# A four-layer selective scan on one core: the gates of a chunk go from VectorE to ScalarE and GpSimd, and the preparation of later chunks gets a new order

## The chip, the cores and the metric

One core of a Trainium2 chip runs the whole program. The metric is the device time of one execution in microseconds (us), the median of three runs. Five engines work side by side, each in the order of its own instruction stream: TensorE (PE, with its weight loads PEld), VectorE (DVE), ScalarE (ACT), GpSimd (POOL) and SyncE (SP), which here issues all DMAs. They are tied together by semaphores only: an instruction that raises a count, and waits for a count ahead of another instruction.

## The reference

The input is 4 sequences of 2048 tokens with 256 features, all in float32. It is normalised, sent through four Mamba layers, added to the input, and sent through a feed-forward part whose operands are quantised to FP4 in blocks. One Mamba layer computes:

```python
xs, z = split(x @ in_w.T)                    # 2 x 512 channels
xc = silu(cb + causal_conv4(xs, cw))
dt, Bm, Cm = split(xc @ xp_w.T)              # 16, 16, 16 columns
delta = softplus(dt @ dt_w.T + dt_b)
h[t] = h[t-1] * exp(delta[t] * A) + (delta[t] * xc[t]) * Bm[t]     # 512 channels x 16 states
y[t] = sum over states of h[t] * Cm[t] + xc[t] * D_skip
x = layer_norm((y * silu(z)) @ out_w.T + x)
```

## The kernel before, in words

**Chunks and steps.** A layer is cut into 16 chunks of 512 tokens (four for each sequence), so the four layers are 64 chunks, counted on as g = 0 to 63. The 512 x 16 states of a chunk are worked in 16 *steps* s = 0 to 15. A step holds four tiles of 128 partitions (32 channels x 4 states) by 512 tokens, and four steps (QS) together give all 16 states of one block of 128 channels, called q. In step s:

- ScalarE, a step ahead, makes `dA` = exp(delta x A) for step s+1 (`exp`, L629), after it has kept the last column of step s-1 (`keep_states`, L638);
- TensorE spreads the B rows over the partitions into the one PSUM bank `B_all` (`broadcast_b`, L456), for step s+1, once VectorE has written both halves of `bu` of step s;
- VectorE multiplies `durep` by `B_all` into `bu` (`times_b`, L1018, two of 1024 columns) and runs four hardware scans (`scan`, L1033). Its order in a step is scan 0, `times_b` second half, scans 1 and 2, `times_b` first half of the next step, scan 3;
- GpSimd multiplies the four states by the C rows into `hc` (`times_c`, L905, two of 1024 columns). `h` and `hc` hold two steps, so the scan of step s+2 waits for `times_c` of step s;
- TensorE, two steps behind, adds `hc` over the states into the PSUM bank `acc` (`sum_states`, L474). In the first step of a block it opens the bank with `skip_term` (L463), the product of `xc` and D_skip, and for that waits until the bank has been read (`acc_read`).

**The gate.** When the four steps of a block are summed, VectorE multiplies `acc` by silu(z) (`gate`, L1039, 128x512). It stands behind scan 0 of steps 6, 10 and 14, and of step 2 of the next chunk.

**The preparation.** Beside these, the engines prepare the chunk to come (n = g+1) and the one after that (g+2), and finish the one before (g-1). Which piece stands in which step is written out by hand in `turn` of each engine. TensorE: last convolution of n in step 0, `project_x` 2, `project_dt` 3 and 4, `project_out` of g-1 5 and 6, `project_in` for z 8 and 9, `transpose_x` of g+2 10, `project_in` for xs 11 and 12, convolutions 13 to 15. ScalarE follows a step later: in steps 0 and 1 the last copies of the convolution, tanh and silu(z), in 4 and 5 the two linear halves of softplus and the sigmoid, in 6 a polynomial (`polynomial`, L724 to L727) that ends with `quad`. GpSimd then has four products of 128x2048: `softplus` 0 (L917) in step 7, 1 (L920) in 8, 2 (L923, gives delta) in 10 and 3 (L927, gives du = delta x xc) in 11. Pieces that pass through the PSUM banks W[0] and W[1] are numbered by `fill`; `w_filled` and `w_read` count by these numbers.

**The transfers.** SP issues, in written order, a store of delta and one of du (1 MB each) to DRAM, and then the loads that replicate their rows over 128 partitions: `load_delta` (into `drep`) and `load_du` (into `durep`, both L309), 4 DMAs of 256 KB for each block q, two blocks in the memory at a time. Block 0 of the next chunk is used by VectorE at the end of step 15 (`times_b` of the next chunk's step 0). `load_x` (L258) brings the tokens of g+2 into the part of `xc` that blocks 0 and 1 of chunk g use, after a step of `sum_states` that shows that they are no longer read.

Of the kernel before, what the change touches and what calls it, by code (L numbers as in the profile page):

```python
# [55 lines left out]
def mamba_layers(nc, x, xbuf, wguT_dram, wdT_dram, w, NL, L, sem):  # L56
# [12 lines left out]
    C_DB, C_CB = 0, DB  # L69

# [7 lines left out]
    with ExitStack() as ctx:  # L78
        def sb(name, shape, dt=F32):
# [79 lines left out]
        acc_read, row_summed, mean_ready, squared, var_ready, lnv_done, guess_ready, newton, root_done, normed, weighted, x_ready = (  # L159
            sem(n) for n in ("acc_read", "row_summed", "mean_ready", "squared", "var_ready", "lnv_done", "guess_ready", "newton",  # L160
# [31 lines left out]
        def outs(n):  # L192

            return 1 if not isinstance(n, int) or n >= 2 else 0

        def fill0(n, name):

            base = 11 * n + 3 if outs(n) else 5 + 10 * n
            if isinstance(n, int) and n == TOT:
                return base - 5  # L200
            return base + {"xp": 0, "dt1": 1, "dt3": 2, "out": 3, "z0": 3 + outs(n), "z2": 4 + outs(n), "tr": 5 + outs(n),
                           "xs0": 6 + outs(n), "xs2": 7 + outs(n), "c0": 8 + outs(n), "c2": 9 + outs(n)}[name]

        def fill1(n, name):

            base = 10 * n + 2 if outs(n) else 4 + 9 * n
            if isinstance(n, int) and n == TOT:
                return base - 4
            return base + {"c3": 0, "dt0": 1, "dt2": 2, "out": 3, "z1": 3 + outs(n), "z3": 4 + outs(n), "tr": 5 + outs(n),
                           "xs1": 6 + outs(n), "xs3": 7 + outs(n), "c1": 8 + outs(n)}[name]  # L210

        FIRST = {"tr": 0, "xs0": 1, "xs1": 1, "xs2": 2, "xs3": 2, "c0": 3, "c1": 3, "c2": 4}

        def fill(b, n, name):

            if name in FIRST:
                if isinstance(n, int) and n == 0:
                    return FIRST[name]
                n = n - 1
            return (fill0, fill1)[b](n, name)  # L220

        LAST_OUT = (fill0(TOT, "out") + 1, fill1(TOT, "out") + 1)

        def out_fill(b, m):

            if isinstance(m, int) and m == TOT - 1:
                return LAST_OUT[b]
            return fill(b, m + 2, "out")
# [19 lines left out]
        def _(sp):  # L248
# [196 lines left out]
        def _(pe):  # L445
# [12 lines left out]
            def skip_term(n, p_, q):  # L458
                if q == 0:
                    pe.wait_ge(skip_w, 16 * layer_of(n) + 16)  # L460
                if positive(DB * n + q):
                    pe.wait_ge(acc_read, DB * n + q)
                pe.matmul(acc[:], skip[:, q, :], xc[:, p_, q, :], start=True, stop=False, skip_group_check=True)  # L463

            def sum_states(at, p_):
# [3 lines left out]
                if s % QS == 0:  # L469
                    skip_term(n, p_, s // QS)  # L470
                for k in range(4):
                    if k % 2 == 0:
                        pe.wait_ge(hc_ready, 2 * G + k // 2 + 1)
                    ins = pe.matmul(acc[32 * k:32 * k + 32, :], gather[:], hc[:, 4 * (s % 2) + k, :], start=False,  # L474
# [97 lines left out]
            for e in range(3):  # L572
# [42 lines left out]
        def _(act):  # L615
# [123 lines left out]

            def squares(m):  # L740
                act.wait_ge(mean_ready, m + 1)
                if positive(m):
# [76 lines left out]
            for e in range(2):  # L819
# [6 lines left out]
            def turn(g, ph):  # L826
                here = ph % 2
                n, other = g + 1, 1 - here
                for s in range(NG):
                    keep_states(group(g, s - 1))  # L830
                    exp(group(g, s + 1), here if s + 1 < NG else other)
                    if not is_last(g):
                        if s == 0:
                            copy_conv(n, other, 2)
                            take_params(n, other)
                        if s == 1:
                            copy_conv(n, other, 3)
                            tanh_xc(n, other)
                    if s == 1:
# [17 lines left out]
                    if not is_last(g):  # L857
                        if s == 9 and is_first(g):
                            act.wait_ge(weights_saved, 48)
                        if s in (9, 10):  # L860
                            copy_z(n, other, 2 * (s - 9))
                            copy_z(n, other, 2 * (s - 9) + 1)
# [5 lines left out]
                    if not is_last(g):  # L868
                        if not (isinstance(g, int) and g == TOT - 2):
                            if s == 11:  # L870
                                copy_xT(g + 2)
                            if s in (12, 13):
# [891 lines left out]
```

## Time and profile before

| what | value |
|---|---|
| median of 3 runs | 8295.75 us (8295.15 to 8297.27) |
| profiled execution | 8298.0 us, span 8296.2 us |
| PE / DVE / ACT / POOL busy | 79% / 95% / 67% / 84% |
| granted TensorE clock, mean | 0.894 of full |
| 64 chunks (first gate at 178.01 us, last at 7564.45 us) | about 116 us a chunk |
| feed-forward part behind them | from about 7600 us to the end |

A row of the timeline begins with its start in us from the span's start and its duration; "x2" behind it means two instructions merged into one row. Neighbouring instructions of an engine overlap a little in the records, so what one costs is read as the distance between starts. Idle time ahead of an instruction stands in brackets with what ended it. Most rows are from chunk 33, whose step 5 begins at 3999.98 us.

### The profile page before, as it was taken

How to read it: one execution, taken by the hardware profiler on the slowest of the kernel's cores; microseconds unless marked ns; L12 is line 12 of the kernel's file. 1: busy time of each engine (PE TensorE's matmuls, PEld its weight loads, DVE VectorE, ACT ScalarE, POOL GpSimd, SP SyncE). 2: the span in 40 equal slices, each digit the busy share in tenths (PEclk: the TensorE clock that was granted, in tenths of full speed). 3: DMA queues.
4: the chain of work that ended last, by engine and by line, in shares of the span. 5: the costliest groups of instructions: out<-in, count | busy, mean ns of one | idle time of the engine just before them, and what ended most of it. 6: DMA issues, size and time to landing. Idle time of an engine off the chain costs nothing. (4 is left out here: it accounts for less than half of the span.)

```text
span 8296.2 us, 75437 instructions
## 1 busy us (share of the span) xinstructions
PE 6530.6 (79%) x21028; PEld 2528.0 (30%) x21028; DVE 7849.2 (95%) x7411; ACT 5545.2 (67%) x9589; POOL 6983.9 (84%) x3444
## 2 busy tenths in 40 slices
PE   5777777787778777787777877887777877775888
PEld 2222222232223222222222322232222322222555
DVE  8999999999999999999999999999999999996776
ACT  5676776777766776667766777667766777663444
POOL 3898889988898888988899888988889888985555
PEclk8989899989989899898999889898999888987999
DMA  6454454444554454554545445454555445451110
GB/s 181 116 118 109 104 127 115 117 115 113 127 118 110 100 121 115 120 122 108 126 115 117 105 109 126 116 125 103 121 119 119 109 104 122 115 118 52 39 38 30
DMA packets 566028, 909.25 MB, mean 110 GB/s; under 512 B 58368, under 2 KB 200192, under 8 KB 564352
## 3 DMA queue, kind: packets, MB, share of 16 engines
q1 hardware_dynamic: 565632, 904.73, 45.7%
q8 instruction: 156, 2.56, 0.1%
q14 instruction: 240, 1.97, 0.1%
HBM read 715.55 MB, written 188.94 MB: 109 GB/s over the span
## 5 line engine op out<-in xcount | busy, mean ns | idle before, releaser
L905 POOL TENSOR_TENSOR hc<-h,crep 128x1024 f32<-128x1024 f32 x2048 | 4782.2, 2360 | 714.3 <-PE acc L474 633.4
L1033 DVE TENSOR_TENSOR_SCAN h<-dA,carry,bu 128x512 f32<-128x512 f32 x3072 | 3755.0, 1264 | 0.4 <-ACT carry L638 0.4
L1018 DVE TENSOR_TENSOR bu<-durep,B_all 128x1024 f32<-128x1024 f32 x2048 | 2480.8, 1211 | 188.2 <-PE B_all L456 168.2
L629 ACT ACTIVATE dA<-drep,cur 128x512 f32<-128x512 f32 x4096 | 2618.7, 711 | 0.6 <-DMA drep<-delta_dram 0.3
L456 PE MATMUL B_all<-dtc,spread_b 128*128 128x512 f32 x2048 | 1308.0, 724 | 1460.8 <-DVE bu L1018 1458.5
L638 ACT COPY carry<-h 128x4 f32<-128x4 f32 x1023 | 199.4, 195 | 1713.0 <-DVE h L1033 1711.6
L474 PE MATMUL acc<-hc,gather 128*32 128x512 f32 x8192 | 1284.9, 703 | 5.5 <-POOL hc L905 5.5
L1033 DVE TENSOR_TENSOR_SCAN h<-dA,bu 128x512 f32<-128x512 f32 x1024 | 1192.4, 1203 | 6.9 <-ACT dA L629 6.8
L498 PE MATMUL work<-xT,inw 128*128 128x512 f32 x2048 | 1119.6, 697 | 93.1 <-ACT xT L649 82.7
L456 PEld LDWEIGHTS B_all<-dtc,spread_b 128*128 128x128 f32 x2048 | 360.0, 208 | 2144.9 <-DVE bu L1018 2057.0
L508 PE MATMUL work<-xs,taps 128*128 128x512 f32 x2048 | 950.3, 607 | 0.0
L498 PEld LDWEIGHTS work<-xT,inw 128*128 128x128 f32 x2048 | 438.2, 226 | 868.0 <-issue 855.8
L508 PEld LDWEIGHTS work<-xs,taps 128*128 128x128 f32 x2048 | 369.1, 190 | 586.0 <-issue 586.0
L536 PE MATMUL work<-outw,sz 128*128 128x256 f32 x2048 | 485.9, 380 | 0.0
L474 PEld LDWEIGHTS acc<-hc,gather 128*32 128x32 f32 x8192 | 171.7, 115 | 934.8 <-issue 731.6
L917 POOL TENSOR_TENSOR quad<-quad,xs 128x2048 f32<-128x2048 f32 x64 | 289.1, 4516 | 170.2 <-ACT quad L727 170.2
L536 PEld LDWEIGHTS work<-outw,sz 128*128 128x128 f32 x2048 | 392.6, 192 | 55.2
L1373 PE MATMUL f_gu<-f_wguT,f_xqT 128*128 128x512 f32 (+1 forms) x768 | 346.6, 605 | 73.5 <-ACT f_xqT L1453 66.5
L910 POOL TENSOR_TENSOR xc<-xc,quad 128x2048 f32<-128x2048 f32 x64 | 289.9, 4530 | 44.3 <-ACT quad L694 44.3
L463 PE MATMUL acc<-xc,skip 128*128 128x512 f32 x512 | 322.8, 718 | 0.0
L927 POOL TENSOR_TENSOR relu<-za,xc 128x2048 f32<-128x2048 f32 x64 | 290.8, 4544 | 0.1
L920 POOL TENSOR_TENSOR quad<-quad,za 128x2048 f32<-128x2048 f32 x64 | 290.7, 4542 | 0.1
(179 smaller groups left out, 6807.8 us busy)
## 6 DMA issues: line engine op xcount, KB each, us to landing
drep<-delta_dram SPq DMA_DIRECT2D x1024, 256.0 KB, 6.4
durep<-du_dram SPq DMA_DIRECT2D x1024, 256.0 KB, 7.2
crep<-c_dram SPq DMA_DIRECT2D x1024, 64.0 KB, 6.7
delta_dram<-za SPq DMA_DIRECT2D x64, 1024.0 KB, 4.2
du_dram<-relu SPq DMA_DIRECT2D x64, 1024.0 KB, 5.3
x_res<-xbuf SPq DMA_DIRECT2D x64, 512.0 KB, 3.8
xbuf<-x_res SPq DMA_DIRECT2D x64, 512.0 KB, 5.4
xc<-xbuf SPq DMA_DIRECT2D x63, 512.0 KB, 4.3
```

The lines of the kernel that those rows point to most:

```text
L456: pe.matmul(B_all[:], spread_b[:, s % QS, :], dtc[:, p_, :], start=True, stop=True).then_inc(bb_ready, 1)
L463: pe.matmul(acc[:], skip[:, q, :], xc[:, p_, q, :], start=True, stop=False, skip_group_check=True)
L474: ins = pe.matmul(acc[32 * k:32 * k + 32, :], gather[:], hc[:, 4 * (s % 2) + k, :], start=False, stop=s % QS == QS - 1, skip_group_check=True)
L498: ins = pe.matmul(W[b][:], inw[:, k, z * DI + e * P:z * DI + (e + 1) * P], xT[:, k, :], start=k == 0, stop=k == KD - 1)
L508: ins = pe.matmul(W[b][:], taps[:, 4 * e + k, :], xs[:, e, k:k + T], start=k == 3, stop=k == 0)
L536: ins = pe.matmul(half, sz[:, p_, k, t * P:(t + 1) * P], outw[:, k, :], start=False, stop=k == DB - 1)
L629: act.activation(dA[:, 4 * (s % 2) + k, :], drep[q % 2][:, k, :], ACT.Exp, scale=cur[:, p_, 4 * s + k:4 * s + k + 1]).then_inc(da_ready, 1)
L905: pool.tensor_tensor(hc[:, pair, :], h[:, pair, :], crep[:, j:j + 1, :].to_broadcast([P, 2, T]), ALU.mult).then_inc(hc_ready, 1)
L927: pool.tensor_tensor(relu[:], za[:], xc[:, p_], ALU.mult).then_inc(du_ready, 1)
L1018: dve.tensor_tensor(bu[:, 2 * k:2 * k + 2, :], durep[q % 2][:, 2 * k:2 * k + 2, :], B_all[:].unsqueeze(1).to_broadcast([P, 2, T]), ALU.mul ...
L1033: dve.tensor_tensor_scan(h[:, r, :], dA[:, r, :], bu[:, k, :], start, ALU.mult, ALU.add).then_inc(scanned, 1)
L1373: ins = pe.matmul(gu[:, at:at + width], xqT[:, t % 2, k, :], wguT[:, k, at:at + width], start=k == 0, stop=k == KD - 1)
```

## The change

Three things change. The gate leaves VectorE: ScalarE copies `acc` into `sums` (`take_sums`) and GpSimd multiplies it by silu(z) from there (its own `gate`, counted by `gated`). The term with D_skip no longer opens the bank; it is added in another step of the block (`SKIP_AT`). The preparation of n and g+2 moves by one step on TensorE (convolution 3 from step 0 to 15 of the turn before, z to 7 and 8, transposes to 9, xs to 10 and 11) and on ScalarE and, for `silu_xc`, on GpSimd; `load_x` waits for a later step of `sum_states`, since block 1 is now read up to step 7. The fill numbers are now counted out in the new order. Cut to its core:

```diff
+    SKIP_AT = (1, 3, 1, 1)
...
             def load_x(n):
-                    sp.wait_ge(summed, 2 * (NG * (n - 2) + QS) + 1)
+                    sp.wait_ge(summed, 2 * (NG * (n - 2) + 2 * QS - 1) + 1)
...
             def load_skip(layer, n):
-                    sp.wait_ge(summed, 2 * NG * n - 6)
+                    sp.wait_ge(summed, 2 * NG * n - 3)
...
             def skip_term(n, p_, q):
-                if positive(DB * n + q):
-                    pe.wait_ge(acc_read, DB * n + q)
-                pe.matmul(acc[:], skip[:, q, :], xc[:, p_, q, :], start=True, stop=False, skip_group_check=True)
+                pe.matmul(acc[:], skip[:, q, :], xc[:, p_, q, :], start=False, stop=False, skip_group_check=True)
...
             def sum_states(at, p_):
-                if s % QS == 0:
-                    skip_term(n, p_, s // QS)
+                q = s // QS
+                if s % QS == 0 and positive(DB * n + q):
+                    pe.wait_ge(acc_read, DB * n + q)
+                if s % QS == SKIP_AT[q]:
+                    skip_term(n, p_, q)
...
             def project_out(m, p_, j):
-                    pe.wait_ge(acc_read, DB * (m + 1))
+                    pe.wait_ge(gated, DB * (m + 1))
...
             def turn(g, ph):     # TensorE
-                        if s == 0:
-                            convolve(nxt, 3)
...
-                        if s in (8, 9):
-                            project_in(nxt, 2 * (s - 8), 1)
-                            project_in(nxt, 2 * (s - 8) + 1, 1)
+                        if s in (7, 8):
+                            project_in(nxt, 2 * (s - 7), 1)
+                            project_in(nxt, 2 * (s - 7) + 1, 1)
-                            if s == 10:
+                            if s == 9:
                                 transpose_x(g + 2)
-                            if s in (11, 12):
-                                project_in(g + 2, 2 * (s - 11), 0)
-                                project_in(g + 2, 2 * (s - 11) + 1, 0)
-                            if s in (13, 14, 15):
-                                convolve(g + 2, s - 13)
+                            if s in (10, 11):
+                                project_in(g + 2, 2 * (s - 10), 0)
+                                project_in(g + 2, 2 * (s - 10) + 1, 0)
+                            if s >= 12:
+                                convolve(g + 2, s - 12)
...
+            def take_sums(n, q):     # ScalarE
+                act.wait_ge(summed, 2 * (NG * n + QS * (q + 1)))
+                if positive(DB * n + q - 1):
+                    act.wait_ge(gated, DB * n + q - 1)
+                squares_ahead = n if q in (1, 2) else n - 1 if q == 0 else min(n, TOT - 1)
+                if positive(squares_ahead):
+                    act.wait_ge(squared, squares_ahead)
+                act.copy(sums[:, q % 2, :], acc[:]).then_inc(acc_read, 1)
...
             def turn(g, ph):     # ScalarE
                     keep_states(group(g, s - 1))
+                    if s == 10 and not is_last(g) and g < TOT - 2:
+                        copy_xT(g + 2)
+                    if s == 2 and not is_first(g):
+                        take_sums(g - 1, DB - 1)
+                    if s in (6, 10, 14):
+                        take_sums(g, (s - 6) // 4)
                     exp(group(g, s + 1), here if s + 1 < NG else other)
                         if s == 0:
-                            copy_conv(n, other, 2)
+                            copy_conv(n, other, 3)
                             take_params(n, other)
-                        if s == 1:
-                            copy_conv(n, other, 3)
                             tanh_xc(n, other)
-                    if s == 1:
+                    if s == 0:
...
                         silu_z(g, here)
...
-                        if s in (9, 10):
+                        if s in (8, 9):
                             copy_z(...)
...
-                            if s in (12, 13):
+                            if s in (11, 12):
                                 copy_xs(...)
...
-                            if s in (14, 15):
-                                copy_conv(g + 2, here, s - 14)
+                            if s >= 13:
+                                copy_conv(g + 2, here, s - 13)
...
+            def gate(n, p_, q):     # GpSimd
+                if q == 0:
+                    pool.wait_ge(z_done, n + 1)
+                pool.wait_ge(acc_read, DB * n + q + 1)
+                pool.tensor_tensor(sz[:, p_, q, :], sums[:, q % 2, :], sz[:, p_, q, :], ALU.mult).then_inc(gated, 1)
...
             def turn(g, ph):     # GpSimd
-                        if s == 2:
+                        if s == 1:
                             silu_xc(g + 1, other)
...
                     times_c(group(g, s))
+                    if s == 2 and not is_first(g):
+                        gate(g - 1, other, DB - 1)
+                    if s in (6, 10, 14):
+                        gate(g, 1 - other, (s - 6) // 4)
...
             def turn(g, ph):     # VectorE
                     scan(at, ph, 0)
-                    if s == 2 and not is_first(g):
-                        gate(g - 1, other, DB - 1)
-                    if s in (6, 10, 14):
-                        gate(g, here, (s - 6) // 4)
                     times_b(at, 1)
```

## Rows read from the trace of the kernel before

**Rows 1.** Costliest groups by line, shapes apart: busy us, mean ns | idle before

```profile
L905 POOL TENSOR_TENSOR hc<-h,crep 128x1024 f32<-128x1024 f32 x2048 | 4782.2, 2360 | 714.3 <-PE acc L474 633.4 <-DMA wdT_dram<-sz 40.3 <-DVE h L1033 34.7
...
L1039 DVE TENSOR_TENSOR sz<-acc,sz 128x512 f32<-128x512 f32 x256 | 170.6, 666 | 6.1 <-PE acc L474 6.1
```

**Rows 2.** Who waited for whom, on VectorE, whole span: total us, times, longest us

```profile
DVE bu L1018 <- PE B_all L456: 168.2, 177, 3.1
...
DVE bu L1018 <- DMA durep<-du_dram: 18.6, 24, 7.7
```

**Rows 3.** Busy time by engine, chunks 32 to 35 (four together)

```profile
sum 465.00, PE 370.40 PEld 136.13 DVE 453.51 ACT 327.37 POOL 414.26; mean PE 92.60 PEld 34.03 DVE 113.38 ACT 81.84 POOL 103.57
```

**Rows 4.** Timeline of VectorE, chunks 32 and 33: start us, us, what

```profile
3961.47 1.23 DVE L1018 TENSOR_TENSOR bu<-durep,B_all 128x1024 f32<-128x1024 f32 x1 [0.22 <-DMA durep<-du_dram]
...
3998.80 2.44 DVE L1033 TENSOR_TENSOR_SCAN h<-dA,carry,bu 128x512 f32<-128x512 f32 x2
...
4002.28 2.44 DVE L1033 TENSOR_TENSOR_SCAN h<-dA,carry,bu 128x512 f32<-128x512 f32 x2
...
4008.11 0.67 DVE L1039 TENSOR_TENSOR sz<-acc,sz 128x512 f32<-128x512 f32 x1
4008.70 1.22 DVE L1018 TENSOR_TENSOR bu<-durep,B_all 128x1024 f32<-128x1024 f32 x1
...
4064.58 2.44 DVE L1033 TENSOR_TENSOR_SCAN h<-dA,carry,bu 128x512 f32<-128x512 f32 x2
...
4077.97 1.21 DVE L1018 TENSOR_TENSOR bu<-durep,B_all 128x1024 f32<-128x1024 f32 x1
...
4107.01 1.23 DVE L1018 TENSOR_TENSOR bu<-durep,B_all 128x1024 f32<-128x1024 f32 x1 [0.56 <-PE B_all L456]
...
4115.10 2.44 DVE L1033 TENSOR_TENSOR_SCAN h<-dA,carry,bu 128x512 f32<-128x512 f32 x2
```

**Rows 5.** Timeline of ScalarE, steps 5 to 10

```profile
4000.11 0.20 ACT L638 COPY carry<-h 128x4 f32<-128x4 f32 x1 [2.00 <-DVE h L1033]
...
4017.99 1.99 ACT L727 ACTIVATE quad<-quad,quad_rest 128x2048 f32<-128x2048 f32 x1
...
4020.68 2.56 ACT L629 ACTIVATE dA<-drep,cur 128x512 f32<-128x512 f32 x4
...
4038.63 1.04 ACT L732 COPY sz<-work 128x512 f32<-128x512 f32 x2
```

**Rows 6.** Timeline of GpSimd, steps 7 to 12

```profile
4020.12 4.52 POOL L917 TENSOR_TENSOR quad<-quad,xs 128x2048 f32<-128x2048 f32 x1 [2.32 <-ACT quad L727]
...
4038.50 9.32 POOL L905 TENSOR_TENSOR hc<-h,crep 128x1024 f32<-128x1024 f32 x4
...
4057.59 4.54 POOL L927 TENSOR_TENSOR relu<-za,xc 128x2048 f32<-128x2048 f32 x1
4062.08 4.67 POOL L905 TENSOR_TENSOR hc<-h,crep 128x1024 f32<-128x1024 f32 x2
```

**Rows 7.** Timeline of the DMA issues of SP, chunk 33

```profile
4012.98 0.40 SPq L258 DMA_DIRECT2D xc<-xbuf  x1
...
4062.15 0.38 SPq L337 DMA_DIRECT2D du_dram<-relu  x1
...
4067.50 1.73 SPq L309 DMA_DIRECT2D durep<-du_dram  x4
```

**Rows 8.** Landing of DMAs: L258, whole span; then L309, 4067 to 4069.4 us

```profile
DMA to landing us min/median/max: 3.8/4.3/6.9
...
DMA to landing us min/median/max: 6.3/7.6/8.7
```

**Rows 9.** Timeline of TensorE, steps 7 to 11

```profile
4023.90 2.07 PE L456 MATMUL B_all<-dtc,spread_b 128*128 128x512 f32 x2 [4.58 <-DVE bu L1018]
...
4049.80 5.80 PE L498 MATMUL work<-xT,inw 128*128 128x512 f32 x8 [1.22 <-ACT xT L649]
...
4057.38 3.70 PE L498 MATMUL work<-xT,inw 128*128 128x512 f32 x8
```

More of the change, by code:

```diff
@@ L69, in mamba_layers @@
     C_DB, C_CB = 0, DB
+    SKIP_AT = (1, 3, 1, 1)
+    FILL_BANK = {"xp": 0, "dt0": 1, "dt1": 0, "dt2": 1, "dt3": 0, "out0": 0, "out1": 1, "tr0": 0, "tr1": 1}
+    FILL_BANK.update({f"{name}{e}": e % 2 for name in ("z", "xs", "c") for e in range(4)})
     xv = xbuf.rearrange("(c t p) d -> c p t d", t=NT, p=P)
@@ L158, in mamba_layers @@
             sem(n) for n in ("da_ready", "bb_ready", "bu_ready", "scanned", "hc_ready", "summed", "carried"))
-        acc_read, row_summed, mean_ready, squared, var_ready, lnv_done, guess_ready, newton, root_done, normed, weighted, x_ready = (
-            sem(n) for n in ("acc_read", "row_summed", "mean_ready", "squared", "var_ready", "lnv_done", "guess_ready", "newton",
+        acc_read, gated, row_summed, mean_ready, squared, var_ready, lnv_done, guess_ready, newton, root_done, normed, weighted, x_ready = (
+            sem(n) for n in ("acc_read", "gated", "row_summed", "mean_ready", "squared", "var_ready", "lnv_done", "guess_ready", "newton",
                              "root_done", "normed", "weighted", "x_ready"))
@@ L190, in is_last @@
             return isinstance(g, int) and g == TOT - 1
[L192 to L202, printed above, removed]
@@ L222, in mamba_layers, with place, place_head @@
-        LAST_OUT = (fill0(TOT, "out") + 1, fill1(TOT, "out") + 1)
+        fill_at, filled = {}, [0, 0]
+        def place(n, *names):
+            for name in names:
+                b = FILL_BANK[name]
+                fill_at[b, n, name] = filled[b]
+                filled[b] += 1
+        def place_head(n):
+            place(n, "tr0", "tr1", "xs0", "xs1", "xs2", "xs3", "c0", "c1", "c2", "c3")
+        place_head(0)
+        place(0, "xp", "dt0", "dt1", "dt2", "dt3", "z0", "z1", "z2", "z3")
@@ new lines, in mamba_layers @@
+        place_head(1)
+        for n in range(1, TOT + 1):
+            if n < TOT:
+                place(n, "xp", "dt0", "dt1", "dt2", "dt3")
+            if n >= 2:
+                place(n - 2, "out0", "out1")
+            if n < TOT:
+                place(n, "z0", "z1", "z2", "z3")
+            if n < TOT - 1:
+                place_head(n + 1)
+        place(TOT - 1, "out0", "out1")
+        def fill(b, n, name):
+            return fill_at[b, n, f"{name}{b}" if name in ("tr", "out") else name]
@@ L224, in out_fill @@
         def out_fill(b, m):
-            if isinstance(m, int) and m == TOT - 1:
-                return LAST_OUT[b]
-            return fill(b, m + 2, "out")
+            return fill(b, m, "out")
         def group(g, s):
@@ L473, in sum_states @@
                         pe.wait_ge(hc_ready, 2 * G + k // 2 + 1)
-                    ins = pe.matmul(acc[32 * k:32 * k + 32, :], gather[:], hc[:, 4 * (s % 2) + k, :], start=False,
+                    ins = pe.matmul(acc[32 * k:32 * k + 32, :], gather[:], hc[:, 4 * (s % 2) + k, :], start=s % QS == 0,
                                     stop=s % QS == QS - 1, skip_group_check=True)
@@ L571, in _ @@
             turn_piece(2)
-            for e in range(3):
+            for e in range(DB):
                 convolve(1, e)
@@ L818, in _ @@
             copy_piece(2)
-            for e in range(2):
+            for e in range(3):
                 copy_conv(1, 1, e)
@@ L857, in turn @@
                     if not is_last(g):
-                        if s == 9 and is_first(g):
+                        if s == 8 and is_first(g):
                             act.wait_ge(weights_saved, 48)
-                        if s in (9, 10):
-                            copy_z(n, other, 2 * (s - 9))
-                            copy_z(n, other, 2 * (s - 9) + 1)
+                        if s in (8, 9):
+                            copy_z(n, other, 2 * (s - 8))
+                            copy_z(n, other, 2 * (s - 8) + 1)
                     if not is_first(g):
@@ L997, in _ @@
             turns(pool, turn)
+            gate(TOT - 1, 1, DB - 1)
             mean(TOT - 1)
@@ L1033, in scan @@
                 dve.tensor_tensor_scan(h[:, r, :], dA[:, r, :], bu[:, k, :], start, ALU.mult, ALU.add).then_inc(scanned, 1)
-            def gate(n, p_, q):
-                if q == 0:
-                    dve.wait_ge(z_done, n + 1)
-                dve.wait_ge(summed, 2 * (NG * n + QS * (q + 1)))
-                dve.tensor_tensor(sz[:, p_, q, :], acc[:], sz[:, p_, q, :], ALU.mult).then_inc(acc_read, 1)
             def work_out_a():
@@ L1154, in _ @@
             turns(dve, turn)
-            m = TOT - 1
-            gate(m, 1, DB - 1)
 class Fp4:
```

22 lines of the change are left out of this document (5 added, 17 removed).

## The prediction

> **What bounds the kernel now.** I read the busy times first. VectorE is busy for 113.4 us of the 116 us of a chunk, GpSimd for 103.6, TensorE for 92.6 and ScalarE for 81.8 [rows 3]; so VectorE is full, and GpSimd, which is to get more work, is nearly so. The waits of VectorE say that in 64 chunks it lost 168.2 us to TensorE's `B_all` and 18.6 us to the DMA that brings `durep` [rows 2]. The second number is small, but it comes 24 times: once 7.7 us at the very start, and 23 times under half a us. A transfer that comes *just* too late, again and again, is one that arrives about when it is wanted also where no wait is shown. That made me look for the chain behind it.
>
> The timeline of VectorE gives its unit: from scan pair to scan pair 3.48 us, so a step is 6.96 us, and a gate costs 0.59 us (4008.11 to 4008.70), not the 666 ns of its record [rows 1, 4]. In the first of four chunks the scans have no carried start and a step is some 0.25 us shorter.
>
> I put t = 0 at the start of step 5 of chunk 33, 3999.98 (the second scan of the pair at 3998.80), and follow the preparation of the next chunk:
> - ScalarE begins at 0.1 with the end of step 4 and then works without a gap until `quad` is ready at 20.0 [rows 5]. GpSimd, which had waited 2.32 us for it, starts its first softplus product at 20.1 [rows 6].
> - From there GpSimd has no idle time: `times_c` of steps 7 to 11, softplus 1 and 2, and softplus 3 last, which ends at 62.1 [rows 6].
> - SP stores du at 62.2 and issues the loads of its block 0 at 67.5 to 69.2 [rows 7]; they land up to 8.7 us after issue [rows 8], and the last of the four, issued some 1.3 us after the first, at about 77.5.
> - VectorE wants this block at 78.0 (4077.97) in chunk 33, half a us later. In chunk 32 it wanted it 0.22 us before it was there (3961.47) [rows 4].
> - From that product to the next step 5 (4116.28, the second scan at 4115.10) are 38.3 us, of them 0.59 for a gate and 0.56 for a stall on `B_all` [rows 4].
>
> So the period of 116.3 us is VectorE's work, but there is a second loop with nearly the same length: step 5, ScalarE, GpSimd, two transfers, VectorE. **Whoever shortens VectorE's work gains only what this second loop also loses.** The change lengthens it.
>
> **The change part by part.** Sums are made against the profiled execution, 8298.0 us, 2.25 us above the median of 8295.75.
>
> *Gates off VectorE.* 256 gates [rows 1] x 0.59 = 150 us of VectorE's stream go, and 2.34 us of each chunk. Were VectorE alone the bound, the time would be 8298 - 150 = 8148. What is late next is the second loop.
>
> *ScalarE's copies.* A 128x512 copy from PSUM costs 0.47 to 0.57 us (two in 1.04) [rows 5]; I take 0.5. The one of step 6 stands ahead of `exp` and the polynomial, in the gapless stretch: `quad` is ready 0.5 us later (bounds 0.47 to 0.6). It also makes `exp` of step 8, which started at 20.7 for a step that VectorE opened at 21.4 [rows 4, 5], come at 21.2 with its first tile ready at 21.9, where VectorE would by then want it at 20.9: a stall of 1 us, so the first gate's gain is lost there. The other three copies lie beside idle time of ScalarE (34 us a chunk [rows 3]).
>
> *GpSimd's products.* A `times_c` of 1024 columns takes 2.33 us in a row of four [rows 6], so a gate of 512 is estimated at 1.17 us; bounds: 1.0 and 1.5. The gate of step 6 fits in the idle 2.32 us ahead of softplus 0 [rows 6]. The gate of step 10 stands ahead of softplus 2: it delays delta and du by 1.17 us. Gates of steps 14 and 2 come behind du.
>
> The trace shows 1024 columns in 2.33 us on GpSimd against 1.12 us on VectorE [rows 4, 6]. The Trainium skill ("GPSIMD Engine Reference", section "Key points") says that VectorE is structurally about twice as fast at elementwise work, which speaks against handing it to an engine that is as full: by that rule the gate would take twice VectorE's 666 ns, 1.33 us, and the sum below would be 10 us higher. The trace agrees with the factor.
>
> *The second loop then.* du is ready at 62.1 + 0.5 + 1.2 = 63.8, its block 0 lands at 79.15. VectorE's remaining way is 38.3 - 0.59 - 0.56 = 37.15 us without stalls, so the period is 79.15 + 37.15 = 116.3: **what it was**. In the chunk whose followers have shorter scans it is 1.2 us less, as before. Without the second loop VectorE would need 116.3 - 2.3 = 114.0 or less; it reaches the product of step 15 at about 78 at the latest, so its stalls of steps 8 to 12 are covered by up to 1.2 us, and what GpSimd or SP loses is not covered at all.
>
> *New order of TensorE.* Convolution 3 leaves step 0 and the skip term leaves step 2, so `B_all` of step 4 comes earlier: of the stall of 0.56 us I keep 0.1 (bounds 0 and 0.6), because two empty steps now follow each other and the granted clock will fall there, as it did after the idle 4.58 us, when `B_all` took 2.07 us [rows 9]. z of step 7 fills the gap that there was, but waits for W[1] (`copy_out` behind `exp`, at 24.4): `B_all` of step 9 ends at 27.4 where 26.6 is wanted, 0.8 us, covered.
>
> *The transposes.* `load_x` now waits for the first pair of `sum_states` of step 7, which TensorE does in its step 9, and the transposes stand directly behind it. With the two stalls above VectorE begins step 9 at 29.7 (21.9 + 6.96 + 0.8); `B_all` follows 2.4 us behind a step's start, then a skip term of 1 us and the pair of 0.5 us: it is summed at 34.7. In the old order SP issued 0.6 us after the pair, and the load takes 4.3 us (3.8 to 6.9) [rows 8]: x is there at 39.6. TensorE waits 4.4 us in its own order, with `B_all` of step 11 queued behind, wanted at 41.3. The idle time is as long as the 4.58 us after which the clock was at half [rows 9]; then transposes end at 41.1 and `B_all` at 43.2: a stall of 1.9 us in VectorE (bounds 0.1, at full clock, and 4.5). xs follows at half clock, as the 5.80 us beside 3.70 shows [rows 9]. VectorE then reaches step 14 at about 66.5 and the product of step 15 at 78.2: covered. But `sum_states` of step 8 ends its first pair at 44.2, and `times_c` of step 10 waits for that; GpSimd wanted it at 43.7 (its row of four at 4038.50 [rows 6], half of it, and the 0.5). That delays du by 0.55, in the slow case. With the fast case at 0, I take 0.3 (bounds 0 and 2.5).
>
> A step of layer loads: `load_inw` (1 MB) must follow x and two replications, at about 40, and the new place wants it at 43 rather than 50. Three layers, 2 us each beyond the cover: 6 us (0 to 25). The skip load and the other weights have a step or more to spare.
>
> *Ends.* The last chunk prepares nothing and gains its 2.3 us; the last gate goes through copy and product, +1.3. Together -1. The feed-forward part is not touched.
>
> *Sum.* 62 loops x (0.0 + 0.1 + 0.3) = +25, layers +6, ends -1: 8298 + 30 = 8328 for the profiled execution, less 2.25 for the median: **8326 us, +0.4%**.
>
> **Rivals.**
> - *The second loop is not closed by the DMA* (a landing that comes earlier as the queue is emptier). Then the next limit is `h`: scan 0 of step 14 (65.8 [rows 4]) needs the first half of `times_c` of step 12, ready at 64.4 [rows 6], a slack of 1.4 us, and becomes 66.1; with `silu_xc` a step earlier GpSimd lets step 3 begin at 101.2, step 5 at 115.1. 62 x 1.1 = 68 us: **8228**. For it: most chunks show no wait on `durep`. Against: the 23 waits, and landings that follow du at a fixed distance.
> - *VectorE stays the bound*: **8146**. Against: GpSimd's stretch of 42 us without a gap.
> - *It cancels*: sum of step 8 in time, no stall in step 3: **8297**. For it: the loop's own sum is exactly zero.
> - *The wait for x decides* (slower too, but much): if x takes over 6 us from the sum, or TensorE's clock is low from step 7 on, each us lies on `times_c` of step 10 and on du, from the point where `sum_states` of step 8 ends after 43.65. 2.5 us x 62: **8450**. For it: the load stands on the path of TensorE's order and has 1 MB of `drep` right behind; against: this load had the same neighbours before and took 4.3 us.
> - *The change doesn't do what it says*, that is, the gates wait for each other through `acc`: the copy of step 6 comes 0.4 us later than the old gate read the bank; nothing more. Held at nothing.
>
> **How the numbers follow.** Forecast (8312 to 8370) 0.37; cancels (8279 to 8312) 0.27; `h` limit and mixtures of it (8200 to 8279) 0.18; VectorE 0.06; the wait for x 0.12. A difference of 0.2% (16.6 us) is what a measurement of this kernel can tell from none. So faster 0.24, same 0.27, slower 0.49. The likeliest case's own range is 8305 to 8370; the range that should hold 8 in 10 takes in the `h` limit down to 8225 and half of the waits for x, to 8390.
>
> **What would show each step right or wrong.** VectorE busy near 7700 us, no L1039; its waits on `durep` grow from 18.6 to some 80 to 120 us and stand in step 15; a gate on GpSimd of 1.1 to 1.3 us; softplus 3 ends 63.5 to 65 after the start of step 5; `exp` of step 8 is waited for, about 1 us a chunk; TensorE waits for `xc<-xbuf` in each chunk, some 4 us; SP's wait in L258 grows. If VectorE's waits are instead on `hc` of GpSimd, the `h` limit is the case; if neither is there, VectorE is the bound; and if the period is over 118 us with `B_all` as the wait, the load of x decides.

## The result and the profile after

| | before | after |
|---|---|---|
| median, 4 runs each on one chip | 8296.2 us (8295.2 to 8297.3) | 8408.1 us (8406.5 to 8410.1) |
| profiled execution, its span | 8298.0, 8296.2 us | 8410.1, 8408.3 us |
| PE / DVE / ACT / POOL busy | 79 / 95 / 67 / 84% | 77 / 92 / 68 / 87% |
| granted TensorE clock, mean | 0.894 | 0.905 |

The ratio is 1.0135 [1.0117, 1.0153]: slower by 112 us, where +30 was forecast, and above the stated range (8225 to 8390). The direction was right, the size was not.

The page of the kernel after, busy us (share of the span) xinstructions, and the waits of VectorE, which answer to [rows 2]:

```profile
PE 6446.4 (77%) x21028; PEld 2531.4 (30%) x21028; DVE 7715.0 (92%) x7155; ACT 5677.2 (68%) x9845; POOL 7293.9 (87%) x3700
```

```profile
DVE bu L1039 <- PE B_all L454: 234.2, 221, 8.6
DVE bu L1039 <- DMA durep<-du_dram: 102.1, 64, 8.0
...
DVE h L1054 <- ACT dA L626: 59.6, 71, 2.0
DVE h L1054 <- POOL hc L915: 45.0, 40, 1.8
```

VectorE lost the work it was to lose. What it does instead is wait: for `durep` in 60 of the 63 chunks behind the first (102.1 us with the start of the program, before 18.6 in 24 waits), and for three engines more than before. Busy time of four chunks, the same stretches as [rows 3]:

```profile
sum 465.00, PE 363.81 PEld 135.11 DVE 438.94 ACT 333.65 POOL 427.44; mean PE 90.95 PEld 33.78 DVE 109.73 ACT 83.41 POOL 106.86
```

No engine is full any more: VectorE is busy for 109.7 us of 116, GpSimd for 106.9. Where none is full and the kernel is slower, a loop through several of them may be the bound. The prediction's second loop can be read from chunk 33, whose step 5 begins at 4058.6 us. TensorE, steps 9 to 11 (answers to [rows 9]):

```profile
4092.68 1.06 PE L473 MATMUL acc<-hc,gather 128*32 128x512 f32 x8
4098.28 1.97 PE L487 MATMUL work<-ident,xc 128*128 128x128 f32 x8 [4.53 <-DMA xc<-xbuf]
4100.04 1.67 PE L454 MATMUL B_all<-dtc,spread_b 128*128 128x512 f32 x2
4101.64 1.07 PE L473 MATMUL acc<-hc,gather 128*32 128x512 f32 x8
```

The transposes wait 4.53 us for x, with `B_all` and the sums of step 8 queued behind. GpSimd, steps 7 to 12 (answers to [rows 6]):

```profile
4079.23 4.53 POOL L933 TENSOR_TENSOR quad<-quad,xs 128x2048 f32<-128x2048 f32 x1 [0.67 <-ACT quad L724]
...
4102.85 4.68 POOL L915 TENSOR_TENSOR hc<-h,crep 128x1024 f32<-128x1024 f32 x2 [0.56 <-PE acc L473]
4107.48 1.27 POOL L922 TENSOR_TENSOR sz<-sums,sz 128x512 f32<-128x512 f32 x1
4108.71 0.21 POOL L952 TENSOR_TENSOR ve<-sq_sum,c_over 128x4 f32<-128x4 f32 x1
...
4118.55 4.54 POOL L943 TENSOR_TENSOR relu<-za,xc 128x2048 f32<-128x2048 f32 x1
```

`times_c` of step 10 starts when the sums of step 8, begun at 4101.64, let it, after 0.56 us without work; then the gate takes 1.23 us (from start to start), and both delay du. SP stores it, loads block 0, and VectorE has it at 4139.60 (answers to [rows 7] and [rows 4]):

```profile
4123.11 0.38 SPq L335 DMA_DIRECT2D du_dram<-relu  x1
...
4128.47 1.73 SPq L307 DMA_DIRECT2D durep<-du_dram  x4
```

```profile
4139.60 1.23 DVE L1039 TENSOR_TENSOR bu<-durep,B_all 128x1024 f32<-128x1024 f32 x1 [2.29 <-DMA durep<-du_dram]
```

Averaged over the 61 periods of chunks 1 to 62, the loop's parts are these, beside what the prediction had put there:

| us | before | forecast | after |
|---|---|---|---|
| step 5 to the start of softplus 0 | 20.13 | 20.6 | 20.61 |
| softplus 0 to softplus 3, start to start | 37.47 | 38.7 (+0.3) | 40.14 |
| softplus 3 itself | 4.53 | 4.5 | 4.54 |
| its end to VectorE's product | 15.78 | 15.35 | 15.72 |
| that product to the next step 5 | 38.16 | 37.15 | 36.93 |
| period | 116.07 | 116.3 (+0.4) | 117.95 |

Such parts add up to the period in any kernel. What tells whether the loop is the bound is how long du's block 0 lies ready before VectorE begins the product: the product began within 0.05 us of the last landing in 60 of 63 chunks of the kernel after and in 34 of 63 of the kernel before, and there in the others up to 0.65 us later (0.42 in chunk 33, from which the prediction was made).

### The profile page after: what moved, and what is told of

It reads as the page before. It is cut to its first block and busy times, and to the rows that moved or that the text cites. A ratio compares the mean times of both kernels' runs of the same rounds, so it can differ in the third digit from the quotient of the medians.

```text
span 8408.3 us, 76140 instructions
## 1 busy us (share of the span) xinstructions
PE 6446.4 (77%) x21028; PEld 2531.4 (30%) x21028; DVE 7715.0 (92%) x7155; ACT 5677.2 (68%) x9845; POOL 7293.9 (87%) x3700
## 5 line engine op out<-in xcount | busy, mean ns | idle before, releaser
L497 PE MATMUL work<-xT,inw 128*128 128x512 f32 x2048 | 976.6, 615 | 263.7 <-ACT x_res L734 162.7
L507 PE MATMUL work<-xs,taps 128*128 128x512 f32 x2048 | 968.3, 616 | 0.0
L454 PEld LDWEIGHTS B_all<-dtc,spread_b 128*128 128x128 f32 x2048 | 379.3, 214 | 1839.3 <-DVE bu L1039 1747.1
L497 PEld LDWEIGHTS work<-xT,inw 128*128 128x128 f32 x2048 | 368.9, 192 | 911.5 <-issue 431.9
L487 PE MATMUL work<-ident,xc 128*128 128x128 f32 x504 | 118.3, 412 | 280.8 <-DMA xc<-xbuf 280.8
L922 POOL TENSOR_TENSOR sz<-sums,sz 128x512 f32<-128x512 f32 x256 | 327.3, 1279 | 0.0
```

The source lines that it names most:

```text
L454: pe.matmul(B_all[:], spread_b[:, s % QS, :], dtc[:, p_, :], start=True, stop=True).then_inc(bb_ready, 1)
L497: ins = pe.matmul(W[b][:], inw[:, k, z * DI + e * P:z * DI + (e + 1) * P], xT[:, k, :], start=k == 0, stop=k == KD - 1)
L507: ins = pe.matmul(W[b][:], taps[:, 4 * e + k, :], xs[:, e, k:k + T], start=k == 3, stop=k == 0)
L922: pool.tensor_tensor(sz[:, p_, q, :], sums[:, q % 2, :], sz[:, p_, q, :], ALU.mult).then_inc(gated, 1)
```

## The experiments

Each kernel was timed beside the kernel before, whose median was 8295.5 to 8295.8 us. Ratios are to it; differences between experiments are those of medians. "After" stands for the kernel after, 8408.1 us. A wait "for step 4" is one that VectorE spent before the product or the scan of step 4; the product of a step stands at the end of the step ahead of it.

### One link of the loop undone at a time

**x_early.** The skip term of block 1 goes to the second step of its block, so that x can be loaded over the block two steps earlier.

```diff
-    SKIP_AT = (1, 3, 1, 1)
+    SKIP_AT = (1, 1, 1, 1)
...
-                    sp.wait_ge(summed, 2 * (NG * (n - 2) + 2 * QS - 1) + 1)
+                    sp.wait_ge(summed, 2 * (NG * (n - 2) + QS + 1) + 1)
```

> The changed kernel with the D_skip term of block 1 added in the block's second step (SKIP_AT 1 instead of 3), so that the load of x waits for sum_states of step 5 instead of step 7; all else is as changed. Theory (a second loop: step 5, ScalarE, GpSimd's softplus products, store and load of du, VectorE's step 15): x is there when TensorE reaches the transposes, sum_states of step 8 is in time, and GpSimd's stretch from softplus 0 to softplus 3 falls from 40.1 to 38.7 us. 62 x 1.4 us and some 10 us at the three layer changes: about 8310 us. Rival (the gate on GpSimd and the copy on ScalarE carry the whole loss, the wait for x is covered): the wait for x goes and the time stays within 15 us of 8408.

Measured: 8321.3 us, 1.0029 [1.0018, 1.0040], 87 us below after (about 8310 was expected). TensorE's 62 waits for x are gone, softplus 0 to 3 is 38.75 us long instead of 40.14, and the three long chunks at the changes of layer (below) are gone too. The late load of x cost 87 of the 112 us. VectorE's waits on `durep` stay at 104.5 us: the loop still closes there, with a shorter period.

**gate12.** The gate of step 10 goes behind softplus 2 and 3.

```diff
-                    if s in (6, 10, 14):
-                        gate(g, 1 - other, (s - 6) // 4)
+                    if s in (6, 12, 14):
+                        gate(g, 1 - other, {6: 0, 12: 1, 14: 2}[s])
```

> The changed kernel with GpSimd's gate of block 1 behind times_c of step 12 instead of step 10, that is, behind the product that gives du. The copy that frees the bank stays where it is. Theory of the second loop: du is 1.23 us earlier in every chunk, 62 x 1.23 = 76 us: about 8332 us, the waits of VectorE on durep fall by as much. Rival (GpSimd's total work or the depth of h is the bound): the same work is done in the chunk, so under 10 us change.

Measured: 8330.2 us, 1.0042 [1.0029, 1.0056], 78 us below after, or 1.26 us a chunk for a product of 1.23. The stretch from softplus 0 to 3 is 38.77 us. GpSimd does the same work in both kernels; only its place ahead of du was dear.

**delta_first.** delta's block 0 is loaded for the next chunk before du is stored, so du's loads no longer stand behind delta's 1 MB; the added wait, for `exp` of step 11, shows that the old block has been read.

```diff
+                    sp.wait_ge(da_ready, 4 * NG * g + 48)
+                    load_delta(n, p_, 0)
                     store_du(n, p_)
-                    load_delta(n, p_, 0)
```

> The changed kernel with the load of delta's block 0 issued ahead of the store of du (with a wait that the old block has been read), so that 1 MB less stands between the store of du and the landing of its block 0. Theory of the second loop: du lands some 4 us earlier, the waits on durep go, and the next limit takes over, the depth of h on GpSimd: scan 0 of step 14 waits for times_c of step 12 at 67.6 us after step 5 and step 3 of the next chunk for times_c of step 1 at 102.6: period 116.4 instead of 117.9, about 8320 us, with waits on hc in place of durep. Rival (the transfer is covered, VectorE waits for it only because it came late for other reasons, B_all is the bound): within 15 us of 8408.

Measured: 8323.1 us, 1.0032 [1.0020, 1.0044], 85 us below after. VectorE's waits:

```profile
DVE bu L1040 <- PE B_all L455: 218.5, 219, 9.6
DVE h L1055 <- POOL hc L916: 80.7, 83, 1.8
...
DVE h L1055 <- ACT dA L627: 47.2, 69, 1.4
...
DVE bu L1040 <- DMA durep<-du_dram: 9.7, 3, 8.3
```

The wait on `durep` has gone, but for 8.3 us at the start of the program, and waits on `hc` have come in its place. The last load of du's block 0 lands 11.9 us after softplus 3 ends, where it took 15.65 after, and lies ready for 0.3 us or more in every chunk. The stretch from softplus 0 to 3 is as long as after (40.05 us) and does not decide any more. What has grown is the wait for GpSimd, through the depth of `h`.

**before_delta_first.** The same edit in the kernel before.

> The kernel before with the load of delta's block 0 ahead of the store of du and nothing else. Theory: the second loop had the length of VectorE's work, so its removal takes the 23 short waits on durep, some 11 us of 8296, and no more, since VectorE is then the bound: about 8285 us. Rival (the landing of du decided every chunk before): 30 us or more.

Measured: 8271.5 us, 0.9969 [0.9957, 0.9981]: 24 us less, 0.4 us a chunk, between what was expected (11) and the rival (30 or more). The block lands 12.0 us after softplus 3 instead of 15.6 and now lies ready for 1.6 us or more in every chunk, so the second loop no longer bounds any, where it had bounded about half. The waits on `durep` fell by 11 us and those on `B_all` by 25 (that of step 13 from 108.4 to 67.4), while those on `hc` grew from nothing to 12. Why `B_all` of step 13 came less late was not settled.

### The parts of the change alone

**order_only.** The new order with the gates still on VectorE.

> The changed kernel with the gates back on VectorE (no copy, no product on GpSimd); the new order of the preparation, the later D_skip term and the later load of x stay. Theory of the second loop: du 1.4 us later through sum_states of step 8, minus what TensorE no longer loses in step 3: +0.5 us a chunk and some 15 us at the layer changes, about 8345 us. Rival (only the gates' move costs): 8296 or less.

Measured: 8351.8 us, 1.0065 [1.0051, 1.0079], +56. TensorE waits for x here as well (62 times), and the three long chunks at the layer changes are there. Softplus 0 to 3 is 1.56 us longer than before, and VectorE's way from the product to step 5 0.67 us shorter.

**gates_only.** The gates moved, the old order of the preparation and the skip term kept.

> The kernel before with only the gates moved (ScalarE's copy ahead of exp, GpSimd's product behind times_c), in the old order of the preparation. Theory of the second loop: quad 0.5 us and du another 1.23 us later, VectorE's way from there 0.59 us shorter, and the 0.5 us of slack that there was used up: +0.8 us a chunk, about 8345 us, with a wait on durep in every chunk and none on x. Rival (the wait for x in the new order does all the harm, the gates alone gain): 8296 - 60 or less.

Measured: 8513.7 us, 1.0261 [1.0247, 1.0275], +218 where some +50 were expected: a miss. VectorE's longest groups of waits, then TensorE's wait for the bank, then ScalarE's timeline in steps 1 and 2 of chunk 33:

```profile
DVE bu L1044 <- PE B_all L456: 486.0, 215, 4.9
...
DVE bu L1044 <- DMA durep<-du_dram: 57.7, 44, 7.2
```

```profile
PE acc L463 <- ACT sums L747: 184.4, 125, 2.5
```

```profile
4086.09 1.28 ACT L687 ACT_TABLE_LOAD   x1
...
4091.24 1.89 ACT L684 ACTIVATE sz<-sz 128x2048 f32<-128x2048 f32 x1
4093.15 1.28 ACT L857 ACT_TABLE_LOAD   x1
...
4094.55 0.58 ACT L747 COPY sums<-acc 128x512 f32<-128x512 f32 x1
```

The copy that frees the bank `acc` in step 2 stands behind tanh, silu and two loads of tables in step 1: it starts 18.9 us after the chunk's step 0, where VectorE's gate had read the bank at 14.9. TensorE waits for the bank in its own order (87.6 us there, and 96.8 in step 6, where ScalarE's gapless stretch has the copy 4.9 us into the step and the gate had been 1.2 us into it), and `B_all` is queued behind. The 486.0 us of waits on `B_all` lie in three places: 178.6 us for step 4 (before 44.3), 118.4 for step 8 (3.3) and 177.3 for step 13 (108.4). Two more kernels test it.

**gates_skip.** As gates_only, and the skip term in step 1 of a block (`SKIP_AT = (1, 1, 1, 1)`), so that less of TensorE's work stands behind the bank.

> The run with the gates moved in the old order, and beside that the D_skip term in the second step of each block, where it doesn't wait for the bank to be read (the load of x waits for sum_states of step 5). That run took 8514 where 8345 was expected, with 486 us of waits on B_all, in steps 3, 7 and 12. Theory: TensorE stands still until ScalarE's late copies of steps 2 and 6 have freed the bank, and what is queued behind that wait (skip term, sums, project_x, B_all) comes late; the skip term is 1 us of it in each of two places: 8514 minus 62 x 1.5 to 2, about 8400 us. Rival (the order of ScalarE's steps 0 and 1 is all of it): 8500 or more.

Measured: 8500.0 us, 1.0246 [1.0232, 1.0260], only 14 us below gates_only where some 110 were expected: a miss, at the value that the rival had named. VectorE's waits:

```profile
DVE bu L1046 <- PE B_all L457: 347.0, 195, 4.8
DVE bu L1046 <- DMA durep<-du_dram: 105.4, 64, 7.3
...
DVE h L1061 <- POOL hc L922: 58.0, 57, 1.3
```

The waits on `B_all` fell by 139 us: for step 8 to 13.7 us and for step 13 to 109.7. So the skip term's place did remove these, but they had been covered for the most part, since du's block came no earlier; 93 us of them came back as waits on `durep` and on `hc` (12.9 us in gates_only). The wait for step 4 stayed at 179.0 us. It lies between the product and the next step 5, where nothing covers it, and that way of VectorE is as long as in gates_only (39.75 us).

**tanh_step1.** The kernel after, with tanh and silu(z) of ScalarE back in step 1, and `silu_xc` of GpSimd in step 2.

```diff
+                        if s == 1:
                             tanh_xc(n, other)
-                    if s == 0:
+                    if s == 1:
...
                         silu_z(g, here)
...
-                        if s == 1:
+                        if s == 2:
                             silu_xc(g + 1, other)
```

> The changed kernel with tanh and silu(z) of ScalarE back in step 1 and GpSimd's silu_xc in step 2, as before; all else, the last convolution in step 15 too, as changed. Theory: ScalarE then comes late to the copy of step 2 (its stretch of tanh and silu is 8 us long), TensorE waits with it, project_x and B_all of step 4 are late by 2 to 3 us in every chunk: 8408 + 62 x 2.5, about 8560 us, the waits on B_all some 150 us more. Rival (that move in the change does nothing): 8408 within 15 us.

Measured: 8642.0 us, 1.0418 [1.0404, 1.0432], 234 us above after; more than was expected (about 155), in the same direction. VectorE waits 471.8 us for `B_all`, 254.0 of them for step 4 (after 7.2). That wait, TensorE's own waits (whole span), and its row for `project_x` in chunk 33:

```profile
DVE bu L1040 <- PE B_all L454: 471.8, 254, 9.6
```

```profile
PE work L514 <- POOL xc L927: 126.9, 64, 11.3
PE acc L473 <- ACT sums L744: 90.5, 111, 1.8
```

```profile
4164.60 6.67 PE L514 MATMUL work<-xc,xpw 128*128 128x512 f32 x8 [1.94 <-POOL xc L927]
```

This is not the copy alone, as the theory had it. In step 2 TensorE waited 34.0 us for the bank (62 times, 0.42 us in chunk 33), but 115.6 us for `xc` from GpSimd, whose `silu_xc` ends 22.5 us after step 0 instead of 16.9; and `project_x`, begun after idle times of TensorE of 3.0, 0.4 and 1.9 us, took 6.67 us in chunk 33 at a granted clock of 0.54 of full (5.9 on average), where after it took 3.70 (4.2). So most of the loss here came through the later `xc` and the lower clock. No run moves the copy alone.

The parts of the loop, mean us over the same periods (softplus 3 itself, 4.5 us in all, is left out), show why the parts of the change don't add:

| us | before | order_only | gates_only | both (after) | tanh_step1 |
|---|---|---|---|---|---|
| step 5 to softplus 0 | 20.13 | 20.13 | 20.78 | 20.61 | 20.61 |
| softplus 0 to 3 | 37.47 | 39.03 | 38.72 | 40.14 | 39.72 |
| end of softplus 3 to the product | 15.78 | 15.82 | 15.79 | 15.72 | 15.71 |
| product to the next step 5 | 38.16 | 37.49 | 39.75 | 36.93 | 40.94 |
| period | 116.07 | 117.00 | 119.59 | 117.95 | 121.53 |

The gates alone cost 218 us, the order alone 56, and both together 112. In the first two rows the costs of the parts add up to within 0.2 us. In the last part they don't: the gates alone lengthen it by 1.59 us, the order alone shortens it by 0.67, and both shorten it by 1.23, because the new order has tanh, silu(z) and `silu_xc` a step earlier, so that TensorE's step 2 waits neither for the bank nor for `xc`.

### The links together

**two** is x_early and gate12; **all3** is these and delta_first.

> The changed kernel with both the early load of x and the gate of block 1 behind step 12. If the two are links of one chain their gains add: GpSimd's stretch back at 37.5 us, only ScalarE's 0.5 us left, period 115.1 us, about 8235 us, faster than before. If another limit (depth of h, B_all) lies close behind, they add to less: 8270 or more.

> All three: early load of x, gate of block 1 behind step 12, load of delta's block 0 ahead of the store of du. Theory: the second loop is clear by 4 us, the depth of h bounds at 114.9 us a chunk and TensorE's stalls stay: about 8225 us, waits on durep near zero. Were VectorE then alone the bound it would be 8150 to 8180; were nothing but du's chain cut, the same as with two.

Measured: two 8250.0 us, 0.9945 [0.9932, 0.9959], where 8235 was expected; all3 8230.2 us, 0.9921 [0.9908, 0.9935], where 8225 was. Two gives 158 us against after, and the single steps 87 + 78 = 165: links of one loop add up. The third then gives 20 instead of 85, which fits a loop that is by now hardly longer than the next limit. In all3 most waits are

```profile
DVE h L1055 <- POOL hc L916: 111.2, 103, 1.8
DVE bu L1040 <- PE B_all L455: 89.0, 145, 2.0
```

on `hc` and `B_all`, and none on `durep` behind the start: the `h` limit, which the prediction had put at 8228. Of the waits on `hc`, 69.1 us are for step 3 and 41.7 for step 14.

**four.** all3, and the gate of block 2 moves from step 14 to step 2 of the next chunk; at its old place GpSimd's `times_c` of step 15 and all behind it stood after it.

```diff
+                        gate(g - 1, other, DB - 2)
                         gate(g - 1, other, DB - 1)
-                    if s in (6, 12, 14):
-                        gate(g, 1 - other, {6: 0, 12: 1, 14: 2}[s])
+                    if s in (6, 12):
+                        gate(g, 1 - other, {6: 0, 12: 1}[s])
```

> The fastest run so far (early load of x, gate of block 1 behind step 12, delta's block 0 ahead of the store of du: 8230 us), and beside that GpSimd's gate of block 2 behind times_c of the next chunk's step 2 instead of step 14. VectorE waits for hc there 103 times, at steps 14 and 3. Theory: the gate of step 14 stands in the chain that releases step 3, not step 14: these waits go by up to 1.2 us a chunk, until step 14 bounds alone: about 8175 us (8160 to 8200). Rival (step 14 holds all of it): 8225 to 8235.

Measured: 8158.5 us, 0.9835 [0.9822, 0.9848], 72 us below all3, a little more than expected (8160 to 8200), and faster than both kernels. The wait on `hc` for step 3 fell from 69.1 to 7.4 us. Page and waits of VectorE:

```profile
PE 6430.7 (79%) x21028; PEld 2493.1 (31%) x21028; DVE 7711.9 (95%) x7155; ACT 5662.5 (69%) x9845; POOL 7286.4 (89%) x3700
```

```profile
DVE bu L1042 <- PE B_all L455: 87.1, 157, 1.3
...
DVE h L1057 <- POOL hc L916: 43.1, 58, 2.3
DVE h L1057 <- ACT dA L627: 42.2, 58, 1.5
```

VectorE is at 95% again and a chunk takes 113.9 us. That is what the prediction had named for VectorE alone (114.0 a chunk; 8146 in all), though waits remain. The busy times of the four engines are those of after to within 0.3% (PEld's apart): with the same work on each engine, place alone makes 250 us.

## Why the prediction was wrong

**What held.**
- The bound. The loop step 5, ScalarE, GpSimd, two transfers, VectorE decides: VectorE begins the product as the block lands in 60 of 63 chunks, the waits on `durep` are 102.1 us (forecast 80 to 120), and three kernels that each take one link out of it win 78 to 87 us.
- ScalarE's copy delays softplus 0 by 0.5 us (20.13 to 20.61).
- The gate on GpSimd takes 1.23 us, start to start, for an estimated 1.17. The Trainium skill ("GPSIMD Engine Reference", section "Key points") has VectorE about twice as fast at elementwise work, which gave 1.33; the record of 1.28 us lies between the two.
- VectorE's way from the product to the next step 5: 37.08 us in chunk 33 (4139.60 to 4176.68), forecast 37.15. Two confirms the sum: its stretch from softplus 0 to 3 is that of before (37.5), softplus 0 is 0.48 later and VectorE's way 1.13 shorter, so the period should fall by 0.65 us; it fell by 0.72.
- The stall on `B_all` of step 11 was put at 1.9 us and is 120.4 us in 62 chunks. That of `exp` of step 8 was put at 1 us and is half of it: 31.8 us in 51 chunks, of the 59.6 us that VectorE waits for `dA` in all. Both are covered by the loop.

**What failed: the term of "The transposes", the wait for x, sized at 0.3 us a chunk and 6 us for the layers; it was 1.4 us a chunk, layers and all.** In chunk 33 its steps came as described, in us from the start of step 5: x's load was issued at 35.1 (forecast 35.3) and had landed at 39.6 (39.6), `B_all` ended at 43.1 (43.2), GpSimd got the sums of step 8 at 44.2 (44.2), and had waited 0.56 us for them (0.55). Two things were wrong. That was taken for the worse of two cases and halved against a case without delay; but the load was late in every chunk (62 waits, 4.5 us each on average). And chunk 33 is one of the mild chunks. In chunk 25 the half clock lasted longer:

```profile
3153.91 1.97 PE L487 MATMUL work<-ident,xc 128*128 128x128 f32 x8 [4.45 <-DMA xc<-xbuf]
3155.67 1.92 PE L454 MATMUL B_all<-dtc,spread_b 128*128 128x512 f32 x2
3157.52 1.91 PE L473 MATMUL acc<-hc,gather 128*32 128x512 f32 x8
```

```profile
3159.58 4.69 POOL L915 TENSOR_TENSOR hc<-h,crep 128x1024 f32<-128x1024 f32 x2 [1.58 <-PE acc L473]
```

`B_all` took 1.92 us instead of 1.67, the sums 1.91 instead of 1.07, and GpSimd waited 1.58. These sums took over 1.5 us in 41 of 61 chunks. GpSimd's wait in that place was 0.15 to 2.2 us over 61 chunks, 1.2 on average and 71 us in all. The prediction had put 1.0 us between the end of `B_all` and the sums that GpSimd wants, which fits chunk 33 but not most others. It had the price in its rival "the wait for x decides" (2.5 us a chunk, 8450); what came is that mechanism at half that price, on top of the forecast case.

The layers' part is the same term. Three chunks took 123.0 to 123.8 us against a median of 117.6, 5.4 to 6.2 us each, and not the 2 that were forecast. TensorE, in the third of them:

```profile
5639.70 5.90 PE L497 MATMUL work<-xT,inw 128*128 128x512 f32 x8 [7.87 <-DMA inw<-in_inw]
```

GpSimd's next `times_c` waited 5.44 us behind that, again ahead of du (3.8 and 3.9 in the other two). With x early, the three chunks are as long as the others. GpSimd's waits in the two places come to 84 us, and x_early, which has none of them, gained 87, where the forecast had put 25.

**A second step failed, the slack ahead of VectorE's product.** The forecast let the first half us of every delay cost nothing, since in chunk 33 of the kernel before the block was there 0.42 us before the product. On average over the chunks it was there only 0.15 us before, and in 34 of 63 the product began as it landed. The prediction had read its 23 waits as "under half a us": that is their mean, eight were longer, up to 1.06 us. The transfer itself did not change: from the end of softplus 3 to the last landing it took 15.62 us before and 15.65 after, on average.

Summed as changes from before, part by part: ScalarE's part came as forecast, the stretch from softplus 0 to 3 grew by 2.67 us where 1.6 was forecast (66 us over 62 chunks), the part with the transfers shrank by 0.06 where 0.5 was forecast (27 us), and VectorE's way shrank by 1.23 where 1.05 was (11 us the other way). That is the 82 us by which the forecast was low. What makes the landing come 15.3 us after softplus 3 in one chunk and 16.6 in another, in either kernel, stays open.

**The rivals.** "It cancels" and the two gains fell, since du came later than in the forecast, not earlier. (By the prediction's own sum the first would be 8295 and not 8297, which changes nothing.) The `h` limit and VectorE's limit were real and rightly priced, but are reached only when the links are taken out: 8230 (8228) and 8158 (8146).

## What to carry to other kernels

A short wait on a transfer that comes back in many passes can be the mark of a loop across engines and queues that is about as long as the full engine's work. Write its parts down as a sum, take each part as a mean over many passes and not from one, and look how long the data lies ready before it is used: that, and not the sum, says whether the loop is closed. Then ask of every piece that is moved whether it stands inside the loop or behind the transfer's start. Work that goes to another engine belongs behind the product that starts the transfer (gate12), and a wait that the loop covers is not worth removing (gates_skip: 139 us fewer waits on `B_all`, 14 us gained). The copy that frees a bank should not stand behind a long stretch, because the in-order engine that wants the bank holds everything behind it (184.4 us of TensorE's waits in gates_only). When the place of a load is changed, look at what stands directly behind its user: after the transposes' 4.5 us of waiting, they and the work behind them ran at half clock.

## What the runs showed of the hardware

- The granted clock after an idle time of 4.5 us: eight transposes of 128x128 took 1.97 us, where the kernel before did them in 1.09 at full clock, and it came back at different points in chunks whose work was the same. Over the transposes, `B_all` and the sums it was 0.51 of full in chunk 25 and 0.65 in chunk 33. `B_all` and the sums behind the transposes took 0.25 + 0.84 us more in chunk 25 than in chunk 33, which is the 1 us between GpSimd's waits of 1.58 and 0.56.
- The same in tanh_step1: after idle times of 3.0, 0.4 and 1.9 us, with 4 us of matmuls between them, eight matmuls of 128x512 took 6.67 us at a granted clock of 0.54, and 3.70 us in the same chunk of the kernel after.
- GpSimd's product of two 128x512 operands took 1.28 us, of 128x1024 2.36 and of 128x2048 4.53, with VectorE 92% busy beside it.
- With delta's loads (4 x 256 KB) out of the way of du's, the store of du and the loads of its block 0 took 11.9 us from the end of softplus 3 to the last landing, on average, instead of 15.65: the store 4.7 us instead of 5.3, the last load 5.9 instead of 9.0. VectorE's waits for du went from 102.1 us to 9.7, of which 8.3 is the start of the program.
